# First-layer-norm statistics and rsqrt seeds moved between passes of a fused attention and mixture-of-experts kernel

## The reference, cut to what matters

```python
def _layernorm(x, axis=-1, eps=1e-05):
    m = jnp.mean(x, axis=axis, keepdims=True)
    v = jnp.var(x, axis=axis, keepdims=True)
    return (x - m) / jnp.sqrt(v + eps)
...
    x = x + _L0_xattn_ref(_layernorm(x, axis=-1), ctx_768, ...)   # 16 heads, 77 keys, D = 512
    x = x + _L0_ffn_ref(_layernorm(x, axis=-1), ...)              # 8 experts, top 2, capacity 1024
    return x
```

## Time and profile before

| what | value |
|---|---|
| runs before | 1439.77, 1442.85, 1443.17 us, median 1442.85 |
| the profiled execution | 1441.63 us, its span 1439.9 us |
| PE, DVE, ACT, POOL busy | 91%, 66%, 56%, 50% of the span |
| granted TensorE clock, mean | 0.966 |

### The profile page before, as it was taken

How to read it: one execution, slowest core, us unless ns; L and a number is a source line. 1 busy time by engine, 2 the same in 40 slices (tenths; PEclk the granted TensorE clock), 3 DMA queues, 4 the chain that set the end, 5 groups by cost and what they waited for, 6 DMA issues and landing times.

```text
span 1439.9 us, 30591 instructions
## 1 busy us (share of the span) xinstructions
PE 1315.5 (91%) x12330; PEld 775.1 (54%) x12330; DVE 955.1 (66%) x1808; ACT 812.6 (56%) x1336; POOL 715.2 (50%) x717
## 2 busy tenths in 40 slices
PE   6458999989998999997849999999999999999996
PEld 3336777767676677764527444444444444444442
DVE  8678898889889787887775545444554545455421
ACT  4558888878998899987455514233251514334210
POOL 3187878777777678876423232242514223241301
PEclk9869999999999999999869999999999999999998
DMA  6147898978887786788433564565546455654401
GB/s 197 52 94 197 205 251 211 230 188 192 204 219 171 181 182 168 183 220 202 132 102 111 168 177 146 154 177 133 163 124 180 141 151 168 156 138 123 105 15 44
DMA packets 319575, 228.89 MB, mean 159 GB/s; under 512 B 253305, under 2 KB 253689, under 8 KB 319434
## 3 DMA queue, kind: packets, MB, share of 16 engines
q1 hardware_dynamic: 304074, 176.28, 49.4%
q0 software_dynamic: 15360, 50.66, 11.9%
HBM read 118.98 MB, written 50.86 MB: 118 GB/s over the span
## 4 chain that ended last, share of the span: by engine, by line
PE 72%; DVE 12%; POOL 7%; issue 4%; ACT 2%; SPq 2%; DMA 1%; DVEq 0%; POOLq 0%; ACTq 0%
PE ps L1213 23%; PE ps L1199 23%; PE ps L1099 8%; PE ps L1029 7%; PE ps L1080 3%; PE ps L1116 2%; POOL sd L542 2%; PE ps L1013 2%; PE ps L1052 1%; DVE x L1486 1%; POOL qT L524 1%; DVE sm L1464 1%; POOL ph L548 1%; PE ps L1002 1%; POOL oT L530 1%
## 5 line engine op out<-in xcount | busy, mean ns | idle before, releaser
L1199 PE MATMUL ps<-xT,w1s 128*128 128x512 f16 (+1 forms) x1632 | 336.5, 369 | 1.9 <-DVE xT L1729 1.5
L1213 PE MATMUL ps<-w2s,hT 128*128 128x512 f16 x1536 | 332.8, 379 | 0.0
L849 ACT ACTIVATE hT<-ps 128x512 f16<-128x512 f32 (+1 forms) x136 | 77.8, 572 | 356.0 <-PE ps L1199 356.0
L1199 PEld LDWEIGHTS ps<-xT,w1s 128*128 128x128 f16 x1632 | 160.6, 99 | 175.5 <-issue 1.9
L1213 PEld LDWEIGHTS ps<-w2s,hT 128*128 128x128 f16 x1536 | 150.2, 98 | 181.3
L593 POOL DMA_INDIRECT out_dram<-ys,idx x64 | 71.4, 1116 | 278.7 <-DVE ys L1769 274.5
L542 POOL TENSOR_TENSOR sd<-sd,rr 128x1232 f32<-128x1232 f32 x64 | 143.9, 2248 | 117.0 <-ACT rr L750 116.9
L1029 PE MATMUL ps<-xnT,wqh 128*128 128x256 f16 x1536 | 194.3, 278 | 5.7 <-ACT partq L732 5.5
L1099 PE MATMUL ps<-woh,oT 128*128 128x512 f16 x768 | 180.2, 384 | 3.7 <-POOL oT L530 3.7
L1759 DVE SCALAR_TENSOR_TENSOR hT<-ps,hT 128x512 f16<-128x512 f32 (+1 forms) x136 | 88.6, 658 | 138.5 <-ACT hT L849 138.4
L1769 DVE SCALAR_TENSOR_TENSOR ys<-ps,gs,og 128x512 f32<-128x512 f32 x64 | 48.1, 751 | 189.7 <-PE ps L1213 189.7
(11 more groups left out here) (206 smaller groups left out, 2012.4 us busy)
## 6 DMA issues: line engine op xcount, KB each, us to landing
xr<-x SPq DMA_DIRECT2D x64, 256.0 KB, 3.6
xrow_dram<-x SPq DMA_DIRECT2D x64, 256.0 KB, 3.7
out_dram<-x SPq DMA_DIRECT2D x64, 256.0 KB, 4.2
stage<-w1T SPq DMA_DIRECT2D x8, 2048.0 KB, 9.5
stage<-w2T SPq DMA_DIRECT2D x8, 2048.0 KB, 8.4
xt<-x SPq DMA_DIRECT2D x59, 256.0 KB, 3.2
xs<-x SPq DMA_DIRECT2D x56, 256.0 KB, 4.2
wqf<-wq SPq DMA_DIRECT2D x1, 1024.0 KB, 7.8
```

The source lines that it names most:

```text
L1199: ins = pe.matmul(hb[z][:, 0:wide], w1s[e % 2][:, a, k, ic * P:(ic + 1) * P], xT[:, 4 * b + k, cols], start=(k == 0 and i == 0), stop=(k = ...
L1213: ins = pe.matmul(yb[z][:, :], hT[:, a, k, s * P:(s + 1) * P], w2s[e % 2][:, b, k, :], start=(k == 0 and i == 0), stop=(k == 7 and i == 2))
```

## The change

`stats_at` keeps its tiles up to pass 15. From there on: no statistics in passes 16 to 23, three tiles (45, 46, 47) in pass 24, two tiles a pass in 25 to 31 (48 to 61), none in 32 to 39, two (62, 63) in pass 40. Since SP's loads follow `stats_at(h + 1)`, they move as well: those of 45, 46 and 47 stand together in SP's pass 23. The seeds of batches 5 to 9 (passes 9, 17, 25, 33, 41) go from behind the statistics to the place between the second half of the sum and the routing steps and `s_recip`. Those of batches 2 to 4 stay.

```diff
@@ stats_at
-            first = 24 + h - 2 + min((h - 1) // 2, 7)
-            return range(first, min(first + 1 + (h % 2 == 0 and h < 16), T))
+            if h < 16:
+                first = 22 + h + (h - 1) // 2
+                return range(first, first + 1 + (h % 2 == 0))
+            if h == 24:
+                return range(45, 48)
+            if 25 <= h < 32 or h == 40:
+                first = 2 * h - 2 if h < 32 else 62
+                return range(first, first + 2)
+            return range(0)
@@ vector, the loop over h
                 if H:
                     next_batch(H[-1])
+                for b in range(5, len(XB)):
+                    if h == seed_at(b):
+                        steps(norm1(b), 9)
                 steps(route, 4)
                 s_recip(h + 5)
                 tx_lo(h + 11)
...
                 for t in stats_at(h):
                     ln1_stats(t)
-                for b in range(2, len(XB)):
+                for b in range(2, 5):
                     if h == seed_at(b):
                         steps(norm1(b), 9)
```

## The result

Nine runs of the changed kernel have a median of 1447.3 us (1444.26 to 1448.72), nine runs of the kernel before 1443.17 (1439.77 to 1445.12). The ratio is 1.0027, 95% interval 1.0019 to 1.0036: 4.1 us slower, just under the 0.3% that I had named as the bound. I had forecast 1442.5 and no change, with 1437 to 1447 as the range; the median lies 0.3 us above it, and the sign of the move was missed. The interval is clear of 1, so the bound of 0.3% was also too coarse: nine runs of each kernel tell 4 us from nothing.

The account below looks back on a forecast made before the run. PE was taken as the bound (91% busy, 72% of the last chain). Terms -1.3 +0.5 -1.5 +3.9 -1.7 +0.5 -1.6 +0.9 sum to -0.3 us against the profiled 1441.63; against the median, 1442.5, range 1437 to 1447.

Parts of the forecast that it names:

- The seeds: Seeds moved to where POOL idles: gains 1.3 (pass 9), 1.7 (25), 1.6 (41); losses 0.5 each in 17 and 33.
- The statistics out of routing passes: Without pass 21's statistics, DVE's L1608 in pass 22 comes just ahead of POOL's L548: gain 1.5 us, other end 0.
- The load wait: Pass 24: third statistics wait 3.3 us for tile 47's load, with two buffers; cost 3.9 us in all.
- the sign I had named: In the changed profile, the four passes from 25 on should take some 37 to 38 us.
- The clock: PE's idle time of some 3.2 us in pass 25 may bring half clock: cost 0.9 us, between 0 and 3.3.
- The load wait is covered: Rival: the third load comes early enough, 4.8 us of cost go; 1437.7 us, faster; chance 0.22.
- DVE becomes the bound from 24 to 31: Rival: two tiles a pass use up DVE's 1.0 us to spare; 1446.7 us, or 1449 with long low clock; chance 0.20.
- The seeds don't meet an idle POOL: Rival: L548 ends after the sum in passes 25 and 41, gains fall to 0.9 each; 1444 us; within the middle case's 0.58.

Follow-up runs that it names:

- e2: Kernel before with only the seeds of batches 5 to 9 moved, statistics as before: median 1443.13 us, ratio 1.0003 to before.
- e4: Changed kernel with the statistics of tile 45 taken in pass 23 instead of 24, so no third load is held: 1443.63 us, ratio 1.0005 to before.
- e5: e4 with the seeds of passes 17 and 33 put back behind the statistics: 1438.09 us, ratio 0.9970 to before.
- e10: Changed kernel with 32 unread matmuls filling PE's idle time in each of passes 19 and 35: 1436.86 us, ratio 0.9959 to before.
- e12: e10 with the four transposes of one tile in pass 14 repeated twice, 0.9 us of added PE work: 1440.37 us, ratio 0.9985 to before.
- e3: Kernel before with only the statistics moved, seeds in their old place: 1447.24 us, ratio 1.0029 to before.
- e9: Kernel before with 32 unread matmuls filling PE's idle time in each of passes 19 and 35: 1441.74 us, ratio 0.9988 to before.
- e1: Kernel before, unedited, run once more: 1442.38 us, ratio 0.9997 to before.
- e11: e5 with 32 unread matmuls filling PE's idle time in each of passes 19 and 35: 1434.40 us, ratio 0.9940 to before.
- e6: e2 with the four transposes of one tile in pass 14 repeated twice, 0.9 us of added PE work: 1443.73 us, ratio 1.0005 to before.
- e7: Kernel before with the four transposes of one tile in pass 14 repeated five times, 2.2 us of added PE work: 1444.37 us, ratio 1.0014 to before.
- e8: Kernel before with only the seeds of pass 9 moved: 1442.26 us, ratio 0.9992 to before.

## Why the prediction was wrong, point by point

**The seeds: right.** Pass 9 brought 1.3 (forecast 1.3), pass 41 1.7 (1.6), pass 25 1.7 once the load wait was gone (1.7, e2 and e4). At 17 and 33 the first seed was held by POOL for 0.5 us as said, and the loss in the passes was 0.3 and 0.6 (0.5 each). With the clock it was more: leaving these two out was worth 5.5 us (e4 to e5). The rule of the Trainium skill that was weighed (GPSIMD Engine Reference, section 1: contention for VectorE instructions in a two-port mode or with two SBUF inputs) fits the trace as far as it goes: the moved seeds take 170 ns where POOL idles, and the held ones end with a POOL instruction. Whether a seed, with one SBUF input, works in a two-port mode is seen in no trace here.

**The statistics out of routing passes: right.** 1.4 for 1.5, all of it in pass 22, where L1615 (L1608 before) came 0.06 us ahead of POOL's L555. That it came ahead at all hung on a margin that small, so part of this is luck. The margin held in every kernel that had the edit.

**The load wait: right in place, a little too dear.** 2.53 us of waiting instead of 3.3, since the load landed some 3.5 us after its release rather than 4.2. Passes 25 and 26 came to +1.8 for my +2.2 (3.9 less the seeds' 1.7); taken alone by e4 the wait is worth 3.7 us of the median. The four passes from 25 on took 41.5 us; the sign I had named, 37 to 38, did not fit my own sum, by which they take 41.9. PE idled for 2.33 us and not for over 3. The median of the rows was 0.7 us too long for this load. The fit in the Trainium skill (DMA: Bandwidth & Descriptors, Anatomy of one DMA) gave 2.6 us, 0.9 too short; it is made there for DMAs issued from GpSimd, and this load is issued by SyncE.

**The clock: this step failed.** I wrote "I take 0.9, between 0 and 3.3", for one new spell in pass 25. It did not come in this profile, nor behind 2.45 and 2.76 us of idle time in e10 and e12, but in e3's it did, 3.4 us long, behind only 2.13 us. What I left out is that the spells already there would change: those in the setup, behind 19, behind 35 and behind 55 were booked as given. In the profiles they carry +7.0 us, against -1.5 from everything else in the attention half. All runs agree in kind: the clock is 0.955 to 0.959 in the nine of the changed kernel and 0.960 or more in every run of before; e2, whose schedule is 3.7 us better than before, measures +0.1; filling two idle stretches turns after against before from +4.1 to -4.9. The price of a spell was right: without the 3.4 and 6.8 us of it, passes 19, 20 and 35, 36 are 1.4 and 3.1 us shorter (e9), for 1.7 and 3.3. The error was to treat the low clock as a fixed cost of before. A change worth 1 to 2 us per place, ahead of several idle stretches that each end in half clock, is not worth its sum.

**The rivals.** *The load wait is covered* (0.22): no, 2.53 us of it stood open. *DVE becomes the bound from 24 to 31* (0.20): no; the four passes from 29 on took 37.1 us as before, with two tiles of statistics instead of one in three of them, and DVE kept 0.19 us or more of idle time before the residuals of passes 27 to 32. That the result lies near that rival's number, 1446.7, is luck: the mechanism is another. *The seeds don't meet an idle POOL*: no.

**Open.** The setup is 0.9 to 2.1 us longer in the profiles of all other kernels than in those with before's exact passes (before, e1, e9), though they issue the same instructions there; with one profile a kernel this may be chance, and 1.1 of the 7.0 us stand there. It is not shown which of the moved seeds and statistics lower the mean clock, and by what way; the seeds of passes 17 and 33 have a part in it (e4 against e5). Nor is it shown why the stretch behind pass 55 changes by up to 4.6 us, only that 0.9 us of work ahead of it can do it (e10 against e12). PE has a third long idle stretch there, in pass 55, of 3.1 to 4.1 us in every profile, which no run filled.

## What to carry to other kernels

List the stretches of low TensorE clock in the profile together with the idle time in front of each; any edit ahead of them can lengthen them, so a gain of a few microseconds should be judged by several medians, or after the idle time has been filled. Filling two idle stretches of 3.5 us with matmuls that nobody reads was worth as much here (3.7 us on the best schedule by the medians of e5 and e11, 4.3 by their distances to before) as the dearest fault of the schedule, the load wait. And before statistics, loads or copies are bunched, count the buffers: with two of them the third in one pass waits for a whole load.

## What the runs showed of the hardware that was not expected

The same idle time of 3.5 us on PE, in the same pass, was followed by no low spell (e5), one of 3.4 us (before, e1, e3, e6) or one of 6.8 us (after, e2, e4, e7, e8). In this pass and in pass 35 the lengths went with the moment at which the clock fell, counted from the end of the idle time, and not with the length of the idle time or its place in the kernel (e5 and e8). A kernel can be slower by 3.5 us for 0.9 us of added work (e12 against e10).

A very small DVE instruction with SBUF operands is held until a long POOL instruction ends. The worst case was the first seed of pass 41 in the kernel before, 2.16 us for an instruction that takes 0.16 in the changed kernel; POOL's L542 ran from 525.89 to 528.14:

```profile
526.01 2.16 DVE L1341 TENSOR_SCALAR nw<-mv 128x8 f32<-128x8 f32 x1
```

If it comes just ahead, it isn't held: whether L1608 comes 0.06 us ahead of POOL's instruction or 0.7 us behind its start decides over 1.7 us.
